# Local attention: q's inverse length moved from a product on q into the exponential's scale and the maxima

## The reference

```python
q, k, v = split(shift_token(x) @ wqkv)          # 8 heads of 64
q = l2norm(q) * qs;  k = l2norm(k) * ksc        # l2norm: t / clip(norm(t), 1e-12)
q, k = rotary_xpos(q, k)                        # turns pairs of channels, by position
# windows of 64 positions; each sees itself and the window before
sim = einsum('bhwid,bhwjd->bhwij', bq * 8, bk)
sim = where(mask, -finfo.max, sim)
out = einsum('bhwij,bhwjd->bhwid', softmax(sim), bv)
```

## Time and profile before

| | us |
|---|---|
| median of 3 runs | 2242.17 (2241.56 to 2242.24) |
| profiled execution | 2243.29 |
| its span (first to last instruction) | 2241.4 |
| mean granted TensorE clock of it | 0.989 |

### The profile page before, as it was taken

The page is one execution under the profiler, slowest core; times in us unless marked ns, Lnnn a source line. Parts: engine busy times, 40 slices in busy tenths (PEclk is TensorE's granted clock), DMA queues, the critical chain, the costliest instruction groups (busy, mean ns, idle before and its releaser), DMA issues.

```text
span 2241.4 us, 53938 instructions
## 1 busy us (share of the span) xinstructions
PE 2125.9 (95%) x19264; PEld 1468.6 (66%) x19264; DVE 1683.1 (75%) x4031; ACT 1541.9 (69%) x4254; POOL 1680.3 (75%) x1712
## 2 busy tenths in 40 slices
PE   6999879999899999899999999999999989999988
PEld 4777557777567777556666656666777756777765
DVE  6777568888568888677677777777888856888865
ACT  3666358888548998626656656657888954889862
POOL 6778779998258888448877787868999834888852
PEclk9999889999999999999999999999999999999999
DMA  4000001112111112121211121111111211111211
GB/s 118 1 1 1 7 21 44 26 41 49 44 32 36 38 39 50 46 67 46 57 46 41 51 58 42 52 27 23 36 32 44 46 45 30 33 38 40 47 31 51
DMA packets 121369, 88.38 MB, mean 39 GB/s; under 512 B 85560, under 2 KB 102160, under 8 KB 118800
## 3 DMA queue, kind: packets, MB, share of 16 engines
q1 hardware_dynamic: 118544, 82.69, 15.3%
q10 hardware_dynamic: 2560, 2.24, 0.4%
HBM read 30.38 MB, written 8.39 MB: 17 GB/s over the span
## 4 chain that ended last, share of the span: by engine, by line
PE 43%; DVE 16%; POOL 14%; issue 5%; SPq 5%; DMA 2%; ACT 1%; POOLq 0%; DVEq 0%
PE bank L1351 11%; POOL store L1163 8%; POOL store L1172 6%; PE bank L1362 5%; PE bank L600 5%; PE bank L1342 5%; DVE store L986 4%; SPq L473 4%; DVE store L991 3%; DVE store L998 3%; PE bank L639 3%; PE bank L730 2%; PE bank L652 2%; PE bank L678 2%; PE bank L614 2%
## 5 line engine op out<-in xcount | busy, mean ns | idle before, releaser
L1575 POOL TENSOR_SCALAR store<-store 128x512 f32<-128x512 f32 x512 | 349.8, 697 | 107.9 <-DVE store L1502 105.9
L1502 DVE CUSTOM_DVE_ANT_0 store<-bank,store 128x512 f32<-128x512 f32 x512 | 335.6, 688 | 120.2 <-PE bank L1342 67.3
L1458 ACT ACTIVATE store<-bank 128x512 f32<-128x512 f32 x512 | 286.8, 600 | 201.5 <-PE bank L1351 198.1
L854 ACT ACTIVATE store<-bank,store 128x128 f32<-128x128 f32 x1024 | 363.4, 375 | 47.9 <-DVE store L1004 47.8
L1163 POOL TENSOR_TENSOR store<-store 128x16 f32<-128x16 f32 x128 | 372.7, 2912 | 27.7 <-DVE store L1000 27.2
L1157 POOL TENSOR_TENSOR store<-store 128x512 f32<-128x512 f32 x256 | 321.2, 1277 | 94.3 <-DVE store L991 90.9
L1351 PEld LDWEIGHTS bank<-store 128*128 128x128 f32 x2048 | 240.1, 142 | 133.5 <-ACT store L1458 75.8
L1351 PE MATMUL bank<-store 128*128 128x128 f32 x2048 | 298.4, 277 | 0.0
L1172 POOL TENSOR_TENSOR store<-store 128x512 f32<-128x512 f32 x256 | 261.7, 1044 | 10.0
L600 PE MATMUL bank<-store 128*128 128x512 f32 x496 | 253.1, 596 | 0.0
L1004 DVE TENSOR_REDUCE store<-bank 128x4 f32<-128x512 f32 x256 | 164.8, 686 | 89.8 <-PE bank L639 89.5
(11 more groups left out here) (224 smaller groups left out, 4556.2 us busy)
## 6 DMA issues: line engine op xcount, KB each, us to landing
store<-store SPq DMA_DIRECT2D x256, 128.0 KB, 2.4
store<-parts SPq DMA_DIRECT2D x96, 192.0 KB
parts<-store SPq DMA_DIRECT2D x16, 384.0 KB, 3.7
store<-store SPq DMA_DIRECT2D x128, 32.0 KB
store<-store SPq DMA_DIRECT2D x128, 31.8 KB
store<-store SPq DMA_DIRECT2D x32, 127.0 KB
store<-in_L_ffn_wqkv_dram SPq DMA_DIRECT2D x4, 768.0 KB, 4.5
out_dram<-store SPq DMA_DIRECT2D x8, 256.0 KB, 2.4
```

Source lines behind the costliest of these rows:

```text
L854: last = nc.scalar.activation(prob[:, e, b, :], bank[3 + e][:, b * P:(b + 1) * P], ACT.Exp, bias=nmax[:, e, b:b + 1], accum_out=psums[:, h ...
L1458: nc.scalar.activation(AT[:, h % 4, c, :], bank[SCORE_BANKS + (64 * q + 4 * h + c) % TURN_BANKS][:, :], ACT.Exp, scale=-1.0).then_inc(aexp ...
L1502: nc.vector.tensor_tensor_reduce(out=S[:, h % 4, t, :], in0=bank[(64 * q + 4 * h + t) % SCORE_BANKS][:, :], in1=decay[:, off:off + L], sca ...
L1575: nc.gpsimd.tensor_scalar(s_, s_, -1.0, amax[:, h % 4, t:t + 1], ALU.mult, ALU.add).then_inc(shifted_done, 1)
```

## The change

GpSimd's product for q is gone: the addition for q writes `roped` itself, and so waits itself for the transpose of the q before. k is treated as before (`normalize_k`). The inverse length of q is used at two other places: each exponential takes it as its scale, one number per partition, from `norm`, and each negative maximum is multiplied by it on DVE, behind a wait for the maximum (new semaphore `peak_done`); the first of the two also waits for `norm_done` of its tile. As the inverse length is now read until the tile's exponentials are done, `norm` has rows for four tiles instead of two.

```diff
--- before.py
+++ after.py
@@ -184,7 +184,7 @@
         turned = mem.take(4, INNER)
         roped = mem.take(2, INNER)
         rope = mem.take(TPS, 2, 2, DH)
-        norm = mem.take(4, H)
+        norm = mem.take(2 * TPS, H)
         qT = mem.take(PAIRS, P)
         kT = mem.take(PAIRS, WIN + L)
         V = mem.take(SLOTS, INNER)
@@ -285,6 +285,7 @@
         y_in = [sem(f"y_in{i}") for i in range(TPS)]
         xT_done, hT_ready = sem("xT_done"), sem("hT_ready")
         qk_done, v_done, sq_done = sem("qk_done"), sem("v_done"), sem("sq_done")
+        peak_done = sem("peak_done")
         ss_done, norm_done = sem("ss_done"), sem("norm_done")
         rot_done, add_done, roped_done = sem("rot_done"), sem("add_done"), sem("roped_done")
         qkT_done, qT_ready, v_ready, tab_ready = sem("qkT_done"), sem("qT_ready"), sem("v_ready"), sem("tab_ready")
@@ -852,7 +853,7 @@
                 for b in range(PAIRS):
                     h = 2 * b + e
                     last = nc.scalar.activation(prob[:, e, b, :], bank[3 + e][:, b * P:(b + 1) * P], ACT.Exp,
-                                                bias=nmax[:, e, b:b + 1], accum_out=psums[:, h:h + 1])
+                                                bias=nmax[:, e, b:b + 1], scale=norm[:, 2 * j, 2 * b + e:2 * b + e + 1], accum_out=psums[:, h:h + 1])
                 last.then_inc(exp_done, 1)
 
             def write_band(q, j):
@@ -993,16 +994,22 @@
 
             def square_sums(q, j):
                 n = 4 * q + j
-                flat = norm[:, 2 * (j % 2):2 * (j % 2) + 2, :].rearrange("p i h -> p (i h)")
+                flat = norm[:, 2 * j:2 * j + 2, :].rearrange("p i h -> p (i h)")
                 dve.wait_ge(roped_done, 2 * n + 2)
                 nc.vector.tensor_reduce(flat, sq[:, :, :].rearrange("p i (h d) -> p (i h) d", d=DH), AX.X, ALU.add).then_inc(ss_done, 1)
                 dve.wait_ge(ss_done, n + 2)
                 nc.vector.tensor_scalar(flat, flat, 1e-24, None, ALU.max).then_inc(clip_done, 1)
 
             def maxima(q, j, e):
-                dve.wait_ge(sim_done, 8 * q + 2 * j + e + 1)
+                n2 = 8 * q + 2 * j
+                dve.wait_ge(sim_done, n2 + e + 1)
                 nc.vector.tensor_reduce(nmax[:, e, :], bank[3 + e][:, :].rearrange("p (b w) -> p b w", w=P),
-                                        AX.X, ALU.max, negate=True).then_inc(max_done, 1)
+                                        AX.X, ALU.max, negate=True).then_inc(peak_done, 1)
+                if e == 0:
+                    dve.wait_ge(norm_done, 4 * q + j + 1)
+                dve.wait_ge(peak_done, n2 + e + 1)
+                nc.vector.tensor_tensor(nmax[:, e, :], nmax[:, e, :],
+                                        norm[:, 2 * j, :].rearrange("p (b u) -> p u b", u=2)[:, e, :], ALU.mult).then_inc(max_done, 1)
 
             def inverse_sums(q, j):
                 dve.wait_ge(exp_done, 8 * q + 2 * j + 4)
@@ -1154,31 +1161,33 @@
             def add_turned(q, j, i):
                 at = 2 * (j % 2) + i
                 pool.wait_ge(rot_done, 8 * q + 2 * j + i + 3)
-                nc.gpsimd.tensor_tensor(straight[:, at, :], straight[:, at, :], turned[:, at, :], ALU.add).then_inc(add_done, 1)
+                if i == 0:
+                    pool.wait_ge(qkT_done, 8 * q + 2 * j + 1)
+                    nc.gpsimd.tensor_tensor(roped[:, 0, :], straight[:, at, :], turned[:, at, :], ALU.add).then_inc(roped_done, 1)
+                else:
+                    nc.gpsimd.tensor_tensor(straight[:, at, :], straight[:, at, :], turned[:, at, :], ALU.add).then_inc(add_done, 1)
 
             def inverse_norms(q, j):
-                flat = norm[:, 2 * (j % 2):2 * (j % 2) + 2, :].rearrange("p i h -> p (i h)")
+                flat = norm[:, 2 * j:2 * j + 2, :].rearrange("p i h -> p (i h)")
                 pool.wait_ge(clip_done, 4 * q + j + 1)
                 hold(pool)
                 nc.gpsimd.tensor_tensor(flat, flat, minus_half[:, 0:2 * H], ALU.pow).then_inc(norm_done, 1)
 
-            def normalize(q, j, i):
-
-                n2, at = 8 * q + 2 * j, 2 * (j % 2) + i
-                if i == 0:
-                    pool.wait_ge(norm_done, 4 * q + j + 1)
-                pool.wait_ge(add_done, n2 + i + 1)
-                pool.wait_ge(qkT_done, n2 + i + 1)
-                nc.gpsimd.tensor_tensor(roped[:, i, :].rearrange("p (h d) -> p h d", d=DH),
+            def normalize_k(q, j):
+
+                at = 2 * (j % 2) + 1
+                pool.wait_ge(norm_done, 4 * q + j + 1)
+                pool.wait_ge(add_done, 4 * q + j + 1)
+                pool.wait_ge(qkT_done, 8 * q + 2 * j + 2)
+                nc.gpsimd.tensor_tensor(roped[:, 1, :].rearrange("p (h d) -> p h d", d=DH),
                                         straight[:, at, :].rearrange("p (h d) -> p h d", d=DH),
-                                        bc(norm[:, at, :], 2, DH), ALU.mult).then_inc(roped_done, 1)
+                                        bc(norm[:, 2 * j + 1, :], 2, DH), ALU.mult).then_inc(roped_done, 1)
 
             def finish_qk(q, j):
                 add_turned(q, j, 0)
                 add_turned(q, j, 1)
                 inverse_norms(q, j)
-                normalize(q, j, 0)
-                normalize(q, j, 1)
+                normalize_k(q, j)
 
             def attention_sequence(s, q, more, norm_more=False):
                 for j in range(TPS):
```

## The result

The changed kernel takes 2370.36 us (median of 4 runs, 2368.18 to 2372.67), beside 2242.20 for the kernel before: ratio 1.0572 (95% interval 1.0554 to 1.0591), slower. The forecast was 2364 us.

A forecast was written before the change was run, and what follows sets the result against it. GpSimd's queue was taken to end last in attention, at 8.364 and 8.472 us a tile. Tiles of 9.41 add 62.8 and 56.3, the last tiles 3: +122 on 2243.3, 2364 us as median; own range 2345 to 2385.

The forecast's parts named there:

- The place of the block: First DVE product of the maxima, issued 0.13 us into GpSimd's product for k, waits for its end, up to 1.04 us.
- ScalarE loop: One attention tile from maxima through exponentials and scores to the next maxima, without blocking: 8.62 us (8.5 to 8.75).
- M: Start of the first maxima of an attention tile, from which the forecast counts its times.
- rival A: First product gets in before k's product, only the second is held: 8.64 us a tile, 2272 us; chance 0.30 with C.
- The loop: Attention tile through DVE product, rotations, clip, power, k's product and the next product: 9.41 us, for 30 tiles per layer and call.
- The tails: Eight last tiles, with no GpSimd work beside them, pay the scales alone, less some slack: 3 us.
- D: More than one block, second product held by GpSimd's additions too, or DVE late: 9.7 to 10 a tile, 2400; chance 0.05.
- T to the next maxima: From the end of the exponentials' last accumulator read (T): band copy, TensorE's start, scores; 2.02 to 2.11 us.
- Product: Each DVE product of the maxima with q's inverse length, 128x4: 0.13 us and a gap of 0.035 behind the reduction.
- Exponentials to T: From the exponentials' start to the end of their last accumulator read: 5.66 us with scales, 4.93 without.
- C: Scales cost as forecast, no product is ever held: 8.62 us a tile, 2270 us; chance 0.30 with rival A.
- B: Scales cost nothing and no product is held: 8.15 us a tile, a gain of 32 us, 2210; chance 0.07.

The follow-up runs named there:

- k_waits: Changed kernel, whole, but GpSimd's product for k also waits for both maxima's products of the tile whose scores run; 2302.89 us, ratio 1.0288.
- k_halves: Changed kernel, whole, but GpSimd's product for k is done in two instructions of 256 columns instead of one of 512; 2320.40 us, ratio 1.0360.
- no_scale: Changed kernel without the exponentials' scale from memory; the two DVE products stay, by a row of ones; 2267.74 us, ratio 1.0133.
- gain_only: Changed kernel without the scale from memory and without the two products of the maxima; 2214.89 us, ratio 0.9888.
- four_scalars: Changed kernel, whole, but each maxima's product is done as four tensor_scalar of one element a partition; 2357.55 us, ratio 1.0528.

## Why the prediction was right

**The place of the block.** A DVE product with two inputs in SBUF, issued while GpSimd's product of line 1172 runs, ends with it: forecast from one operation on one number a partition, shown by the time line after and by k_waits, k_halves and no_scale. Forecast were 0.13 us between the two starts, measured 0.29; the margin was larger than feared, as two terms of the ScalarE loop were too small. There was some luck in that: without a hold (k_waits) the product comes 9.63 us after the last M where 9.34 was forecast, and k's product would start at 9.35 where 9.21 was; errors as large the other way would have brought rival A.

**The loop.** 9.41 us a tile forecast, 9.44 measured; 119 us over 120 tiles, measured 121.5 over the 124 distances. The tails and the rest: 3 forecast, 6.8 measured. D didn't come: the second product takes 0.16.

**Mis-sized terms, none of which moved the result.** T to the next maxima: 2.06 forecast, 2.26 measured; I took the band copy to be last, but TensorE's transposes begin 0.48 after T (848.54 to 849.02) and the scores 1.12 after it. Product: 0.13 and a gap of 0.035, measured 0.16 and 0.11. Exponentials to T: 5.66, measured 5.58; the scale adds 0.09 to the distance of two exponentials, as the earlier trace rows gave, and it is the stretch without scale that is shorter (4.86 in gain_only, 4.93 in the earlier trace rows). With k_waits the loop of ScalarE is 8.83, so the rivals A and C were priced at 2272 and 2270 where the same sum gives 2295 with 8.83, and the run gave 2303.

**The rivals.** B's gain is there (25 us measured, 32 forecast) but needed both costs to be nothing. That free scales with blocking would still be slower, at 8.64 a tile, was said there and measured in no_scale.

**A sign that was wrong.** I said GpSimd would still be in the chain. It has 1% of it, and ScalarE 11%: a DVE operation that is held counts as busy DVE from its issue, and who holds it stands nowhere. In the next tile the same hold is written as 0.47 us idle after the maxima. Only laying GpSimd's row beside DVE's shows it.

**The rule on the shared pair.** That GpSimd's instruction keeps the pair to its end (the Trainium skill, SBUF — State Buffer, SBUF: two separate sides) agrees for the dense products, and k_halves shows it by instruction. For the power it doesn't: in no_scale 122 products with two SBUF inputs began inside the power, and each took its plain 0.16 or 0.17 us. The forecast had this from line 970, whose operations have one tensor input only. The same section of the Trainium skill names two SBUF inputs or a two-port mode as the condition; four_scalars, not held, and the clip, held, agree only if the first is outside that mode and the second in it, and no run here shows the mode.

## What to carry to other kernels

Work taken off the engine that ends the chain (here 130 us of GpSimd, worth 25) pays only up to the next loop; add up that loop with the replacement's cost in it, 0.09 us for each scale from memory included. Before a small DVE operation out of SBUF goes between two engines (two inputs, or one like the clip), lay it on the time line against GpSimd's long additions and products: where it starts inside one, its price is the rest of that instruction, whatever its own size, and the whole queue behind it pays. Compare variants with the tiles at the same addresses: a scratch tile of 32 bytes cost 21 us here.

## What was not expected of the hardware

- 32 bytes a partition of shift: issues of a one-partition transfer from SBUF to SBUF 7.40 us in the median instead of 6.55, 21 us of the kernel; 128 and 160 bytes cost nothing. Not explained.
- A DVE product with two SBUF inputs passes through GpSimd's power (2.91 us) unhindered.
- The first tiles of an attention in the changed kernel differ: in layer 2 the first two powers stand 10.7 us apart and the next two 6.7 or 6.9. Scale and products aren't the cause of that, since gain_only has it too (10.73 and 6.71). Open are the 10.6 and 10.2 of two attentions behind these, which gain_only doesn't have, and single tiles of up to 9.8 later on, each followed by one of 8.6 or 8.7. A version that computes all of the reference and keeps the 25 us was not found.
